# Asking for the third pair's weights between the stores of the first pair's halves

## The reference

```
x = x + L0_xattn(layernorm(x), ctx, Wq, bq, Wk, bk)
x = x + L0_ffn(layernorm(x), A, B, Wr)                       # top 2 of 4 experts, rank 16
x = x + L1_xattn(layernorm(x), ctx, ctx, mask, wq, wk, wv, wo)   # 32 query heads, 8 key heads of 128, rotary
x = x + L1_ffn(layernorm(x), route_w, A, Bw)                 # top 1 of 8 experts, rank 16
...
q = (query @ wq).reshape(bs, sq, HQ, DK).transpose(0, 2, 1, 3)
q = apply_rope(q, pos)
```

## Time and profile before

| | |
|---|---|
| median of 3 runs | 1742.9 us (1741.88 to 1745.31) |
| profiled execution | 1745.47 us, its span 1743.6 us |
| TensorE busy | 1711.9 us, 98% of the span |
| VectorE, ScalarE, GpSimd busy | 1118.3 us (64%), 769.2 us (44%), 888.3 us (51%) |
| mean granted clock of TensorE | 0.996 |

### The profile page before, as it was taken

The page is one execution under the profiler, slowest core; times in us unless marked ns, Lnnn a source line. Parts: engine busy times, 40 slices in busy tenths (PEclk is TensorE's granted clock), DMA queues, the critical chain, the costliest instruction groups (busy, mean ns, idle before and its releaser), DMA issues.

```text
span 1743.6 us, 26099 instructions
## 1 busy us (share of the span) xinstructions
PE 1711.9 (98%) x8784; PEld 1560.6 (90%) x8784; DVE 1118.3 (64%) x2200; ACT 769.2 (44%) x1609; POOL 888.3 (51%) x687
## 2 busy tenths in 40 slices
PE   7999999999999999999999999999999999999998
PEld 6999999999888888888989999889999999999986
DVE  7631176556632333334968888898888888888845
ACT  5211211002332232223322233488888888878724
POOL 3224523114622221221487874488787887878734
PEclk9999999999999999999999999999999999999999
DMA  4122333224743334432244445577777777777643
GB/s 135 61 61 84 122 122 103 82 90 142 215 130 116 113 120 129 130 112 74 88 142 113 118 130 150 140 209 198 191 191 191 192 192 192 193 192 193 163 109 108
DMA packets 177199, 241.37 MB, mean 138 GB/s; under 512 B 47313, under 2 KB 145873, under 8 KB 176065
## 3 DMA queue, kind: packets, MB, share of 16 engines
q1 hardware_dynamic: 177088, 239.99, 49.4%
HBM read 142.68 MB, written 46.92 MB: 109 GB/s over the span
## 4 chain that ended last, share of the span: by engine, by line
PE 80%; DVE 4%; POOL 2%; issue 2%; DMA 1%; ACT 1%; SPq 0%; DVEq 0%; ACTq 0%; POOLq 0%
PE bank L200 76%; PE bank L106 1%; PE bank L2605 1%; PE bank L186 1%; PE bank L2618 1%; POOL shared_operand_low L329 1%; DMA aw_weights_then_ctx_rows<-in_wk 1%; DVE q_crossed L859 0%; DVE q_crossed L858 0%; POOL w_rest_low L794 0%; POOL w_first_low L1612 0%; PE bank L1287 0%; DVE e_scores L1985 0%; DVE q_rotated_then_x_rows L1674 0%; PE bank L1284 0%
## 5 line engine op out<-in xcount | busy, mean ns | idle before, releaser
L329 POOL TENSOR_TENSOR shared_operand_low<-ctx_raw,shared_operand_high 128x768 fp32r<-128x768 f32 x64 | 119.4, 1878 | 200.0 <-ACT shared_operand_high L325 200.0
L200 PE MATMUL bank<-shared_operand_high,w_first_high 128*128 128x448 f32 (+1 forms) x568 | 206.1, 363 | 1.4 <-DVEq L810 0.7
L200 PE MATMUL bank<-shared_operand_high,w_first_low 128*128 128x448 f32 (+1 forms) x568 | 205.3, 361 | 0.0
L200 PE MATMUL bank<-shared_operand_low,w_first_high 128*128 128x448 f32 (+1 forms) x568 | 205.2, 361 | 0.0
L1993 ACT ACTIVATE e_scores<-e_scores,e_least 128x375 f32<-128x375 f32 x256 | 153.6, 602 | 36.1 <-DVE e_least L1985 35.7
L325 ACT ACTIVATE shared_operand_high<-ctx_raw 128x768 fp32r<-128x768 f32 x64 | 52.9, 843 | 212.3 <-DMA ctx_raw<-in_ctx_t 194.0
L1985 DVE CUSTOM_DVE_ANT_0 e_scores<-bank,e_mask_then_layer_ffn 128x375 f32<-128x375 f32 x256 | 134.8, 529 | 0.0
L200 PE MATMUL bank<-shared_operand_high,w_rest_high 128*128 128x376 f32 x384 | 128.8, 335 | 0.9 <-POOL w_rest_low L794 0.9
L200 PE MATMUL bank<-shared_operand_high,w_rest_low 128*128 128x376 f32 x384 | 128.6, 335 | 0.0
L200 PE MATMUL bank<-shared_operand_low,w_rest_high 128*128 128x376 f32 x384 | 128.6, 335 | 0.0
L2028 DVE STREAM_TRANSPOSE q_rotated_then_x_rows<-e_scores 128x768 f32<-128x768 f32 x128 | 124.1, 970 | 0.3 <-DVE e_scores L2006 0.3
(11 more groups left out here) (324 smaller groups left out, 5080.4 us busy)
## 6 DMA issues: line engine op xcount, KB each, us to landing
ctx_raw<-in_ctx_t SPq DMA_DIRECT2D x64, 384.0 KB, 3.9
e_shuffled_then_xn_t<-q_rotated_then_x_rows SPq DMA_DIRECT2D x128, 192.0 KB, 3.6
e_shuffled<-q_rotated_then_x_rows SPq DMA_DIRECT2D x128, 192.0 KB, 3.7
e_raw_wo<-in_wo SPq DMA_DIRECT2D x64, 256.0 KB, 3.9
aw_weights_then_ctx_rows<-in_wq SPq DMA_DIRECT2D x30, 512.0 KB, 4.5
q_rotated<-q_rotated_then_x_rows SPq DMA_DIRECT2D x64, 224.0 KB, 2.4
e_raw_then_a<-q_rotated SPq DMA_DIRECT2D x64, 224.0 KB, 3.8
v_rows<-v_out SPq DMA_DIRECT2D x48, 256.0 KB, 2.5
```

Source lines behind the costliest of these rows:

```text
L200: mm = pe.matmul(out, stationary[a], moving[b], start=(first and i == 0), stop=(last and i == 2))
L329: pool.tensor_tensor(k.ctx_ring[1][slot][:, 2 * j:2 * j + 2, :], k.c_raw[:, j % 2], f32(k.ctx_ring[0][slot][:, 2 * j:2 * j + 2, :]), ALU.s ...
```

## The change

The two requests for the third pair's weights (`load_w(1, 0)` and `load_w(1, 1)`) move in SyncE's queue: the first to the place between the second and the third store of pair 0, the second between the third and the fourth. The waits for older transfers stay where they were, and so now stand behind these requests. Everything else is the same.

```diff
         load_w(0, 0)
         load_w(0, 1)
         for unit, (t, h) in enumerate(FIRST):
+            if unit >= 2:
+                load_w(1, unit - 2)
             store(unit, 0, t, h)
         for t in range(2):
             sp.wait_ge(q1.v_stored[t], 16 + 16 * 3 * BATCH)
             sp.wait_ge(q1.x_out[t], 16 + 16 * BATCH // 2)
         for s in k.k_stored:
             sp.wait_ge(s, 16 + 16 * BATCH * GROUPS // 4)
-        for t in range(2):
-            load_w(1, t)
         for t in range(2):
             for h in range(2):
                 store(4 + 2 * t + h, 1, t, h)
```

## The result

| | before | after |
|---|---|---|
| median, us (6 runs each, same chip) | 1742.28 | 1747.32 |
| lowest to highest, us | 1741.33 to 1745.31 | 1746.25 to 1749.56 |
| ratio, with its 95% interval | | 1.0027 [1.0018, 1.0037] |
| span of the profiled execution, us | 1743.6 | 1747.8 |

The kernel is slower by 5.0 us, about 0.3%. The prediction was 1746.2 us, so the side is right, the range holds the time, and the sum is 1.1 us short (as a difference +3.3 us was said and +5.0 measured, 1.7 us short: the kernel before came out at 1742.28 here, not 1742.9).

The account below looks back on a forecast made before the run. TensorE, busy 98% of the span, was taken as the bound, with the late weight request on the path to the end. GpSimd's 4.0 - 0.91 + 0.17 = 3.3 us on 1742.9 gave 1746.2 us, range 1741.5 to 1748.8.

Parts of the forecast that it names:

- Requests and landing, cost 0: SyncE's moved requests wait for nothing; tiles land at about 850.6 and 855.6, before GpSimd is free at 857.00; cost 0.
- Turns, one instruction each, 1.64 us: VectorE's eight subtractions and GpSimd's instructions alternate, 1.64 us a turn; subtractions end at 870.6 in place of 861.76.
- Rival 1: VectorE's queued subtractions go one behind another, GpSimd starts at 861.7 as before: 1742.9 us; 0.12 together with weights landing late.
- rival 2: GpSimd and VectorE do not exclude each other; GpSimd works from 857.03: 4.0 us faster, 1738.9 us; chance 0.12.
- TensorE's first idle time, 6.1 us, and +1.9 us net: TensorE waits 6.1 us for the subtractions before "first"; after savings and clock, +1.9 us at "sixth" of the fourth pair.
- The store of unit 7 holds back the mask and the tiles: VectorE's late unit 7 delays its store in SyncE's queue, so the mask is requested at about 878.9, tiles directly behind.
- The stream of 2.5 MB in 8.8 us: Mask and fourth pair's two tiles in one stream, 7.4 + 1.4 us, landing 887.7; GpSimd's fourth pair +4.0 us.
- The ring hands the delay on at the twelfth pair: GpSimd and its loads, slightly slower than TensorE, pass on 4.0 - 0.91 + 0.17 = 3.3 us at the twelfth pair.
- TensorE's lead of 2.35 us: Time in hand at the fourth pair between GpSimd's low "sixth" ending (891.31) and TensorE needing it (893.66): 2.35 us.
- the short waits that I expected in the late pairs: TensorE waits of 0.1 to 0.4 us for GpSimd's low parts, forecast for the changed kernel's profile.

Follow-up runs that it names:

- experiment 4: Changed kernel, with GpSimd waiting for VectorE's eight subtractions before its first weight sum of the third pair: 1743.09 us, 1.0003.
- experiment 8: Changed kernel, mask requested ahead of pair 1's stores, eight subtractions split in two fours, straight part of pair 1's rotations left in PSUM: 1739.93 us, 0.9981.
- experiment 1: Changed kernel, with the mask requested behind both weight tiles of the fourth pair: 1743.54 us, 1.0003 against the kernel before.
- experiment 2: Changed kernel, with the mask requested ahead of the four stores of pair 1: 1743.83 us, 1.0005 against the kernel before.
- experiment 6: Kernel before, without early requests, with the mask requested right in front of the fourth pair's second tile: 1746.00 us, 1.0023.
- experiment 10: As experiment 8, but with the mask in its old place behind the stores of pair 1: 1743.26 us, 1.0009 against the kernel before.
- experiment 7: Changed kernel, mask requested ahead of pair 1's stores, eight subtractions split, four in front of units 3 and 4, four behind: 1741.84 us, 0.9992.
- experiment 9: As experiment 8, but with both tiles and the mask requested behind the first pair's four stores: 1744.07 us, 1.0005 against the kernel before.
- experiment 5: Changed kernel, with only tile 0 requested between the stores and tile 1 back behind all four: 1746.22 us, 1.0016.

## Why the prediction was right, step by step

- *Requests and landing, cost 0.* Right: 845.55 and 850.23, and GpSimd didn't wait for a transfer.
- *Turns, one instruction each, 1.64 us.* Right: 12.95 us for eight, 1.62 us each. They ended at 869.7, where 870.6 was said: they began at 856.74, 0.66 us before, and met GpSimd's last x part first, and the sum had added VectorE's 0.4 us once more behind eight full turns (857.03 + 8 x 1.64 is 870.15). Rival 1 (VectorE keeps its turn) and rival 2 (no exclusion) fall here, and experiment 4 shows that GpSimd is the cause. By the Trainium skill (SBUF — State Buffer, Who interferes with whom) a VectorE instruction with two inputs in SBUF contends with a GpSimd one that reads SBUF, for a port pair that is locked, and one with at most one input in SBUF does not. These 1.62 us agree with the first, and the additions of experiment 8 with the second: 0.62 us with an input in PSUM, the one at 865.49 beside a GpSimd that is busy throughout.
- *TensorE's first idle time, 6.1 us, and +1.9 us net.* Size wrong. It was 4.33 us, because the subtractions ended 0.9 us earlier and TensorE came 0.75 us later; net about +0.5, and nothing that can be told from no change in experiments 1 and 2 (+0.6 and +0.9 us by the medians, both intervals hold 1).
- *The store of unit 7 holds back the mask and the tiles.* Right: 878.16, said 878.9.
- *The stream of 2.5 MB in 8.8 us.* Mis-sized: from 878.16 to the landing at 888.7 it was 10.5 us. Most of this lies in a reading of the kernel before. The 7.4 us to 878.3 were the mask's alone, and the first tile landed 6.5 us after its request, at 879.4. The kernel before, SyncE's timeline and then issues and landing (KB, us):

```profile
872.93 0.35 SPq L1468 DMA_DIRECT2D aw_weights_then_ctx_rows<-in_wq  x1
```

```profile
e_mask_then_layer_ffn<-in_mask SPq DMA_DIRECT2D x1, 1500.0 KB, 7.4
aw_weights_then_ctx_rows<-in_wq SPq DMA_DIRECT2D x1, 512.0 KB, 6.5
```

So 2.0 MB took 8.6 us, and with the same 1.4 us for the rest the sum would have been 10.0. GpSimd's fourth pair began at 888.83, +5.0 us, where +4.0 was said. Experiments 1, 2, 6 and 10 show that this stream is what costs.
- *The ring hands the delay on at the twelfth pair.* This is the step that failed, though its sum came out near. With my sizes nothing would have shown at the fourth pair: 4.0 us of delay less TensorE's lead of 2.35 us is under TensorE's own 1.9 us. With the measured ones (5.0 of delay, 0.5 of its own) about 2 us were short at once: TensorE idled 1.97 us before that pair's first product, and its clock fell again. From there on the low part of "sixth" leads by 0.5 us or more in each of the pairs up to the twelfth, so the ring isn't binding, and the short waits that I expected in the late pairs are not there; at the twelfth pair TensorE is 4.17 us late (1034.47 against 1030.30), no more than at the fourth. The ring does bind in experiment 8, with leads of 0.16 to 0.18 us in three pairs. That was the bound that rival 2 worked out (1738.9, for the change without the collisions); 1739.93 was reached.
- *Total.* Said +3.3 us, measured +5.0 [+3.1, +6.4 by the ratio's interval]. The 4.3 us of the trace are 0.5 (turns), 2.13 (idle time, start to start) and 1.6 (clock). How much of the 1.6 belongs to every execution stays open, see below. That the total came out as near as this is in part luck: the loss was expected at the twelfth pair and arose at the fourth, by a landing 1 us later than said and a fall of the clock that was not in the sum. The prediction itself gave a loss that a measurement can tell 0.40, and no difference that it can tell 0.48.

## What to carry to other kernels

Before a load is asked for earlier, look at what the engine behind it would have done meanwhile and which other engine it would meet in that time: GpSimd's idle time was what let VectorE run at three times the pace. And ask of every engine that gets late which requests stand behind its stores in a queue: here a 1.5 MB transfer that nobody awaited soon was pushed in front of the tiles that the next pair needed. An early load pays (here 3 us) once the two are taken apart, by the order of work, by an operand left in PSUM and by moving the big load out of the stream. With the last alone, and with either the second or the last left out, no gain was shown (experiments 2, 7 and 10).

## What was not expected of the hardware

- The turns are strict over eight instructions: neither engine got two in a row, though both had more work waiting (but for 0.16 us in which GpSimd waited for ScalarE). GpSimd's 1.27 us became 1.67, VectorE's 0.54 became 1.62.
- A 512 KB tile requested close behind the 1.5 MB mask landed 8.6 to 9.6 us after its request (changed kernel, experiments 6 and 10), and about 4 us without it. In the kernel before the first tile, requested 2.1 us behind the mask, took 6.5: in every case it landed after the mask.
- TensorE's clock doesn't follow from the length of the idle time alone. It stayed at 1.00 behind idle times of 1.01, 1.38, 1.63, 2.13 and 2.58 us (experiments 7, 8, 9 and 5), and fell to 0.50 (1.2 GHz) behind 1.97 (changed kernel), 2.73, 2.99 and all longer ones. How long it stays down varies too: 3.4 us in experiment 1, 6.8 in the changed kernel and in experiment 2, around the same 4.3 us of idle time. What sets either was not tried; with one profile of each kernel, 1 to 3 us of each trace's account hang on it.
